# Attention's pipeline one step shorter, its normalisation moved within VectorE's step, in a fused attention and mixture-of-experts kernel on one Trainium2 core

## What is computed

```python
# x, ctx: (64, 64, 128); 16 heads of 8; 8 experts, hidden 512
q, k, v = proj(layernorm(x), Wq, bq), proj(ctx, Wk, bk), proj(ctx, Wv, bv)
q, k = rope(q), rope(k)
p = softmax(where(mask == 0, -1e9, q @ k.T / sqrt(8)))
x = x + tanh(g_xattn) * ((p @ v) @ Wo.T + bo)

z = layernorm(x)
logits = z @ Wr + br
e = argmax(logits);  gate = softmax(logits)[e]
x = x + tanh(g_ffn) * gate * (gelu(z @ W1[e] + b1[e]) @ W2[e] + b2[e])
```

## Time and profile before

| | |
|---|---|
| median of 3 runs | 305.37 us (304.95 to 306.65) |
| the profiled execution | 306.31 us, its span 304.5 us |
| mean granted clock of TensorE | 0.945 of full |
| PE busy | 244.9 us, 80% of the span |
| PEld busy | 210.9 us, 69% |
| DVE busy | 191.4 us, 63% |
| POOL busy | 181.8 us, 60% |
| ACT busy | 166.4 us, 55% |

### The profile page before, as it was taken

The page is one execution under the profiler, slowest core; times in us unless marked ns, Lnnn a source line. Parts: engine busy times, 40 slices in busy tenths (PEclk is TensorE's granted clock), DMA queues, the critical chain, the costliest instruction groups (busy, mean ns, idle before and its releaser), DMA issues.

```text
span 304.5 us, 10523 instructions
## 1 busy us (share of the span) xinstructions
PE 244.9 (80%) x3529; PEld 210.9 (69%) x3529; DVE 191.4 (63%) x639; ACT 166.4 (55%) x481; POOL 181.8 (60%) x222
## 2 busy tenths in 40 slices
PE   1458799997998878888889868869568999999960
PEld 1246687786787766777768656758458899999960
DVE  5546777988798799977797784645623443334420
ACT  2155688886787775778678661342503344444410
POOL 7466567567478875688968764056463455544450
PEclk9999999997999999999999995897787999999995
DMA  7711465464344734152422213310323322100100
GB/s 222 213 17 31 99 199 137 98 174 122 94 140 112 194 68 127 20 151 39 145 44 44 43 39 94 80 41 33 93 87 96 106 67 62 51 29 30 37 19 0
DMA packets 58535, 26.63 MB, mean 87 GB/s; under 512 B 38608, under 2 KB 53989, under 8 KB 58484
## 3 DMA queue, kind: packets, MB, share of 16 engines
q1 hardware_dynamic: 55204, 20.15, 26.9%
q0 software_dynamic: 2272, 4.46, 4.4%
q10 hardware_dynamic: 1008, 1.35, 1.5%
HBM read 16.70 MB, written 5.51 MB: 73 GB/s over the span
## 4 chain that ended last, share of the span: by engine, by line
PE 39%; DVE 13%; issue 13%; POOL 12%; SPq 7%; ACT 6%; DMA 4%; another core or an unknown queue 4%; POOLq 1%; DVEq 0%; ACTq 0%
PE ps L745 11%; SPq L406 5%; PE ps L788 4%; PE ps L729 3%; POOL rot L545 3%; POOL rot L539 3%; PE ps L803 2%; POOL rot_s L541 2%; PE ps L727 2%; PE ps L728 2%; DMA kbd<-kT 2%; DVE mx L1210 2%; PE ps L778 2%; PE ps L830 2%
## 5 line engine op out<-in xcount | busy, mean ns | idle before, releaser
L560 POOL DMA_INDIRECT out<-fin,got x39 | 37.8, 970 | 40.5 <-DVE fin L1259 28.5
L1210 DVE TENSOR_REDUCE mx<-ps 128x16 f16<-128x1024 f32 x32 | 39.1, 1222 | 18.5 <-PE ps L803 14.5
L745 PE MATMUL ps<-w_f,hT 128*128 x312 | 47.5, 298 | 0.0
L512 POOL DMA_INDIRECT rows<-x_all,dest_i x32 | 33.2, 1037 | 21.9 <-DVE x_all L1060 14.7
L1259 DVE SCALAR_TENSOR_TENSOR fin<-ps,got 128x128 f32<-128x128 f32 x39 | 13.7, 350 | 49.2 <-PE ps L745 34.6
L745 PEld LDWEIGHTS ps<-w_f,hT 128*128 128x128 f32 x312 | 40.2, 202 | 1.2 <-issue 0.2
L788 PE MATMUL ps<-vx,pr 128*64 128x32 f32 x1024 | 37.6, 228 | 4.1 <-ACT pr L589 1.7
L788 PEld LDWEIGHTS ps<-vx,pr 128*64 128x64 f32 x1024 | 34.1, 143 | 8.0 <-issue 2.8
L589 ACT ACTIVATE pr<-ps 128x1024 f32<-128x1024 f32 x32 | 32.7, 1022 | 9.4 <-PE ps L830 9.0
L539 POOL TENSOR_TENSOR rot<-qk,cf 128x256 f32<-128x256 f32 x32 | 23.4, 732 | 22.6 <-ACT qk L609 16.0
L657 ACT ACTIVATE hT<-ps 128x512 f32<-128x512 f32 x39 | 23.3, 597 | 22.6 <-PE ps L729 15.3
(11 more groups left out here) (156 smaller groups left out, 606.9 us busy)
## 6 DMA issues: line engine op xcount, KB each, us to landing
kbd<-kT SPq DMA_DIRECT2D x128, 32.0 KB
got<-rows SPq DMA_DIRECT2D x39, 72.0 KB
w_f<-in_W_rows SPq DMA_DIRECT2D x8, 256.0 KB, 2.9
w_r<-in_W_last_row SPq DMA_DIRECT2D x8, 256.0 KB, 3.3
w_f<-in_L_ffn_W SPq DMA_DIRECT2D x8, 256.0 KB, 5.0
x_all<-in_x SPq DMA_DIRECT2D x3, 512.0 KB, 4.9
xt_all<-in_x_t SPq DMA_DIRECT2D x3, 512.0 KB, 4.4
ct_all<-in_ctx SPq DMA_DIRECT2D x3, 512.0 KB, 4.3
```

Source lines behind the costliest of these rows:

```text
L512: pool.indirect_dma_start(out=rows, out_offset=bass.IndirectOffsetOnAxis(ap=dest_i[:, t:t + 1], axis=0), in_=x_all[:, t, :], in_offset=Non ...
L560: pool.indirect_dma_start(out=out_d, out_offset=bass.IndirectOffsetOnAxis(ap=got_i[:, u % GOT, R_ID:R_ID + 1], axis=0), in_=fin[:, u % FRI ...
L745: mm = pe.matmul(o, hT[:, par, c, :], w2_f[:, bass.ds(e, 1), c, :].rearrange("p o n -> p (o n)"), start=False, stop=(c == FC - 1))
L1210: dve.tensor_reduce(mx[:, t % 2, 0:H], ps_s[:, :].rearrange("p (h k) -> p h k", k=S), AX.X, ALU.max).then_inc(mx_done, 1)
```

## The change

Attention's tail is a step shorter: the pair (L1142, L1145) of tile t, its transpose, copy and output projection are in step t+4, with pv, and the output addition and statistics in step t+5. On VectorE the pair moves from ahead of L1155 to behind the statistics L1178 and ahead of the routing pieces. `GROUP_AT` is a step earlier (10, 17, 24, 31, 36), and the scatters with it; F0 stays at 34. The expert number of a tile is worked out ahead of the second layer, a step sooner, and held in a register. The second layer waits for `f_fin` only for the first six tiles and the last. The output bias (once, in step 4) moves ahead of its first use.

```diff
         def out_step(u):
-            return F0 + 5 + u // 2 if u < 3 else min(max(SCATTER_AT) - 2 + u, STEPS - 1)
+            return F0 + 4 + u if u < 2 else min(max(SCATTER_AT) - 1 + u, STEPS - 1)
...
-        GROUP_AT = {b - 1 + 6: g for g, (a, b) in enumerate(GROUPS)}
+        GROUP_AT = {b - 1 + 5: g for g, (a, b) in enumerate(GROUPS)}
...
-        SCATTER_AT = {**{i: 1 for i in (*range(15, 21), *range(22, 32))}, 32: 4, 36: 3, 37: 2, 38: 2, 41: 3, 42: 2}
+        SCATTER_AT = {**{i: 1 for i in (*range(14, 20), *range(21, 32))}, 32: 3, 35: 3, 36: 2, 37: 2, 40: 3, 41: 2}
...
 # ScalarE
-                t = i - 5
+                t = i - 4
                 if live(t):
                     act.wait_ge(onT_done, t + 1)
...
 # TensorE
-                experts[u] = (words[v // PACK] >> (3 * (v % PACK))) & 7
+                experts[u] = pe.snap((words[v // PACK] >> (3 * (v % PACK))) & 7)
...
             def rows_transposed(u):
-                expert_numbers(u)
...
             def second_layer(u):
-                wait(pe, f_fin, used(y_bank, u))
+                if u < 6 or u == NS - 1:
+                    wait(pe, f_fin, used(y_bank, u))
...
             def step(i):
-                t = i - 5
+                t = i - 4
                 if live(t):
                     pe.wait_ge(on_done, t + 1)
...
-                t = i - 5
+                t = i - 4
                 if live(t):
                     pe.wait_ge(onT_ev, t + 1)
                     pe.matmul(ps_op, pick, c_h[:, :], start=True, stop=False)
                     pe.matmul(ps_op, onT[:, t % 2, :], wo_x[:, :], start=False, stop=True).then_inc(op_done, 1)
+                if tile(i - F0):
+                    expert_numbers(i - F0)
                 if tile(i - F0 - 2):
                     second_layer(i - F0 - 2)
...
 # VectorE
-                t = i - 5
-                if live(t):
-                    dve.wait_ge(pv_done, t + 1)
-                    dve.reciprocal(rden[:, t % 2, :], o_ps[:, :, HD]).then_inc(rden_done, 1)
-                    dve.tensor_tensor(on[:, t % 2, :]...)
                 t = i
                 if live(t):
                     dve.scalar_tensor_tensor(out=qk[:, t % 2, 0:D], in0=ps_q, ...)
...
-                t = i - 6
+                t = i - 5
                 if live(t):
                     dve.bn_stats(st6b[:, t % 2, :], x_all[:, t, 0:D]).then_inc(bn2_s, 1)
                     dve.bn_aggr(x_all[:, t, R_MEAN:R_MEAN + 2], st6b[:, t % 2, :]).then_inc(bn2_a, 1)
+                if i == 4:
+                    output_bias_halves()
+                t = i - 4
+                if live(t):
+                    dve.wait_ge(pv_done, t + 1)
+                    dve.reciprocal(rden[:, t % 2, :], o_ps[:, :, HD]).then_inc(rden_done, 1)
+                    dve.tensor_tensor(on[:, t % 2, :]...)
                 if i in GROUP_AT:
                     route_var(GROUP_AT[i])
```

More of the change, by code:

```diff
@@ L806, in step @@
                     mm.then_inc(s_done, 1)
-                t = i - 5
+                if i == 4:
+                    pe.wait_ge(s_prep, 5)
+                    pe.wait_ge(s_wow, 2)
+                    pe.wait_ge(s_idw, 1)
+                    pe.matmul(bank[4][:, P:P + QX], c_bc[:, :], id_wr[:, :], start=True, stop=True).then_inc(s_c, 1)
+                t = i - 4
                 if live(t):
-                    if t == 0:
-                        pe.wait_ge(s_cs, 2)
                     pe.wait_ge(on_done, t + 1)
@@ L834, in step @@
                 if i - 2 in GROUP_AT:
-                    if live(i - 5):
-                        pe.wait_ge(onT_ev, i - 4)
+                    if live(i - 4):
+                        pe.wait_ge(onT_ev, i - 3)
                     else:
@@ L839, in step @@
                     rank_of(GROUP_AT[i - 2])
-                t = i - 5
+                t = i - 4
                 if live(t):
+                    if t == 0:
+                        pe.wait_ge(s_cs, 2)
                     pe.wait_ge(onT_ev, t + 1)
@@ L852, in step @@
                     pe.transpose(ps_mx, mx[:, t % 2, :], ident_h).then_inc(mxT_done, 1)
-                if i == 4:
-                    pe.wait_ge(s_prep, 5)
-                    pe.wait_ge(s_wow, 2)
-                    pe.wait_ge(s_idw, 1)
-                    pe.matmul(bank[4][:, P:P + QX], c_bc[:, :], id_wr[:, :], start=True, stop=True).then_inc(s_c, 1)
             pipeline(step)
@@ L1136, in step @@
                                       ).then_inc(f_lo, 1)
-                t = i - 5
-                if live(t):
-                    dve.wait_ge(pv_done, t + 1)
-                    wait(dve, on_done, t - 1)
-                    o_ps = ps_o.rearrange("p (h c) -> p h c", c=16)
-                    dve.reciprocal(rden[:, t % 2, :], o_ps[:, :, HD]).then_inc(rden_done, 1)
-                    dve.wait_ge(rden_done, t + 1)
-                    wait(dve, onT_done, t - 1)
-                    dve.tensor_tensor(on[:, t % 2, :].rearrange("p (h d) -> p h d", d=HD), o_ps[:, :, 0:HD],
-                                      rden[:, t % 2, :].rearrange("p (h o) -> p h o", o=1).broadcast_to([P, H, HD]),
-                                      ALU.mult).then_inc(on_done, 1)
                 t = i
@@ L1178, in step @@
                     dve.bn_aggr(x_all[:, t, R_MEAN:R_MEAN + 2], st6b[:, t % 2, :]).then_inc(bn2_a, 1)
+                if i == 4:
+                    output_bias_halves()
+                t = i - 4
+                if live(t):
+                    dve.wait_ge(pv_done, t + 1)
+                    wait(dve, on_done, t - 1)
+                    o_ps = ps_o.rearrange("p (h c) -> p h c", c=16)
+                    dve.reciprocal(rden[:, t % 2, :], o_ps[:, :, HD]).then_inc(rden_done, 1)
+                    dve.wait_ge(rden_done, t + 1)
+                    wait(dve, onT_done, t - 1)
+                    dve.tensor_tensor(on[:, t % 2, :].rearrange("p (h d) -> p h d", d=HD), o_ps[:, :, 0:HD],
+                                      rden[:, t % 2, :].rearrange("p (h o) -> p h o", o=1).broadcast_to([P, H, HD]),
+                                      ALU.mult).then_inc(on_done, 1)
                 if i in GROUP_AT:
@@ L1227, in step @@
                     output_bias()
-                if i == 4:
-                    output_bias_halves()
                 if i == 20:
```

## The result

The changed kernel takes **313.21 us** (median of 4 runs, 312.66 to 314.08); the kernel before, on the same chip, 305.9 us. The ratio is 1.022, 95% interval 1.015 to 1.029: slower, as forecast, and by 7.3 us where 4.4 were forecast. The profiled execution took 312.66 us with a span of 310.8 us, 6.3 more than before's 304.5.

What follows compares the result with a forecast made beforehand. The prediction took a loop of waits to bound attention and TensorE the expert layers. Attention +9.3, joint -2.0 and expert tiles -2.9 gave +4.4 us: 309.8 us from a median of 305.37, range 303 to 316.5, the forecast's own 307 to 313.

Steps and rivals of the forecast that it cites:

- the loop that the forecast called tight: Attention: stack transposes, pv, score matmuls, VectorE's maximum, casts and GpSimd's L526 form one gapless loop of 4.76 us in step 8.
- No engine in the loop rests between its input and its start: Attention loop, step 8: anything put between pv's end and the maximum lengthens the step by its own length.
- The pair and the statistics behind pv: VectorE in attention: the pair adds 0.5 us a step (14.0 us), input statistics about 0.45 us (10.0 us), before deductions.
- TensorE's next halt takes it in: nothing: TensorE in attention: the product's transpose starts later, but the halt at the maximum's transpose absorbs it; cost nothing.
- stay at about 5: Attention sign: plain steps without input statistics (24 on) stay at about 5 us; those with go from 4.8 to 5.3.
- Routing pieces: VectorE in attention's routing steps: operations behind the pair cost 2.7 us per group, 8.3 us in all before deductions.
- Rival 2: Routing operations stretch inside GpSimd's rotation, adding 4 to 7 us: 314 to 317 us; sign L973, L1001 over 1 us; chance 0.17.
- The attention sum of +9.3: Attention: work put between pv's end and the maximum, 33.7 us, less what already lay there, leaves +9.3 us.
- The joint, -2.0: Between attention and expert tiles: one attention step fewer saves 2.0 us, between 1.0 and 2.9.
- One wait per expert tile: TensorE's second layer: one semaphore wait fewer saves 0.09 us for 32 tiles, -2.9 us, ends 0 and -4.8.
- The clock, rival 3: Longer TensorE halts in attention's routing steps lose its clock, 4 us more: 313 to 314 us; chance 0.08.
- no one's: Joint: the rest of TensorE's stop has no cause in the waits; a shrink over 5 us would prove this wrong.

Runs made afterwards that it cites:

- 9, swap: Kernel before with ScalarE's copy of the transposed maximum (L595) moved ahead of the exponential (L589); ratio to before 1.003 (1.000 to 1.006).
- experiment 6: Kernel before with VectorE's reciprocal and product for the step's own tile right in front of the maximum, TensorE's order untouched; ratio 1.015 (1.008 to 1.022).
- experiment 1: Changed kernel with reciprocal and product moved behind input statistics and routing pieces, right in front of the maximum; 1.025 of before, 299.2 us against 291.5.
- experiment 7: Kernel before with the step's own reciprocal and product ahead of routing pieces and input statistics, TensorE's order untouched; ratio 1.021 (1.016 to 1.025).
- experiment 8: Kernel before with TensorE's transpose of the product (L815) also waiting for ScalarE's third value copy (L637); ratio 1.015 (1.010 to 1.021).
- 2: Kernel before with only the second layer's wait on the final sum left out where it is implied; ratio 0.990 (0.985 to 0.994).
- 3: Kernel before with VectorE's routing pieces also waiting for the step's pv, reciprocal and product left at the step's head; ratio 1.014 (1.009 to 1.018).
- 12: Changed kernel with its late scatters spread over steps 35 to 42 and held until their step's tile is reached; 1.017 of before (1.010 to 1.024).
- 4: Kernel before with GpSimd's 16 late row scatters spread over steps 36 to 43 and held for their step's tile; ratio 0.996 (0.993 to 1.000).
- 10: Kernel before with expert-tile wait left out, late scatters spread, and ScalarE's copy ahead of the exponential, all together; ratio 0.983 (0.977 to 0.989).
- 11: Kernel before with late scatters spread over steps 36 to 43, run again in a third set; ratio 0.994 (0.990 to 0.997).

## Why the prediction was right, and where it was not

**Two paths, not one.** The stack transposes L778 wait for both GpSimd's L526 and ScalarE's copy L595. From L778's start to the end of the pv behind it are 1.66 us (56.12 to 57.78). Ahead of L778 stand two paths, and the runs of step 8 give both (us, from the rows above and the earlier trace rows; the L815 of before started at 53.39, the swap's L815 and maximum at 53.98 and 54.09, and experiment 6 has them at 53.94 and 54.11 and L778 at 56.66):

| kernel | product's transpose to L778 | maximum to L778 | step, L778 to L778 |
|---|---|---|---|
| before | **2.73** | 2.62 | 4.76 |
| changed | **2.73** | **2.45** | 5.08 |
| 1, pair last | **2.72** | 2.85 | 5.07 |
| 6, pair last, TensorE untouched | **2.72** | 2.55 | 4.76 |
| 7, VectorE's half | 3.05 | **2.46** | 5.08 |
| 8, TensorE's half | **2.70** | 3.07 | 5.21 |
| 9, swap | 2.59 | **2.48** | 4.62 |

In each row the path that is at its shortest (bold) is the one that sets the step; the other has slack. (In the swap the transpose's path is shorter than elsewhere, since the copy no longer stands behind the exponential.) In the kernel before it was the transpose's: 0.37 us behind pv, plus 2.73, plus 1.66, is 4.76. The maximum's would have allowed 0.48 + 2.46 + 1.66 = 4.60, the length of steps 22 and 29; with the transpose's path shortened by the swap, step 8 comes to 0.48 + 2.48 + 1.66 = 4.62. So the loop that the forecast called tight had 0.16 us of slack, and another path, which it did not see, had none. In the changed kernel they are level: 0.69 + 2.73 + 1.66 = 5.08 and 0.97 + 2.46 + 1.66 = 5.09. This is why undoing one of them alone gave nothing.

The forecast's points in its order:

- **"No engine in the loop rests between its input and its start"** failed for L778. The profile names L526 as its releaser; L526 ended at 55.88 and L595 at 55.86. TensorE started 0.26 us after L595. In experiments 1 and 8, where L526 had long been done, it is 0.25 and 0.26; behind L526 it is 0.10 in the changed kernel, in 7 and in 9. Two releasers 0.02 us apart are no evidence for either.
- **The pair and the statistics behind pv**: right in length (0.97 us, experiment 7 too). The first 0.16 us put there cost nothing, because of that slack: 0.33 us for 0.49. Experiment 7 alone gives 6.1 of the 7.6 us that the maximum of step 31 is later.
- **"TensorE's next halt takes it in: nothing"** is the step that failed in mechanism. TensorE has no halt there to give: the sixteen matmuls behind the transpose feed the exponential. Alone it would cost 0.32 us in a plain step (experiment 8: 0.45 for 0.47). In steps with input statistics it cost nothing on top, since VectorE's path had become as long. In steps 28 to 30, which have none, it sets the step by itself: the maximum starts only 0.54 to 0.66 us behind pv, yet from L778 to L778 they take 5.07 or 5.08 us, 4.93, 4.76 and 4.84 before (experiment 7: 4.76 and 4.75 in steps 29 and 30). The profile names the copy there:

```profile
174.70 1.22 DVE L1214 TENSOR_REDUCE mx<-ps 128x16 f16<-128x1024 f32 x1
174.73 0.33 PE L818 MATMUL ps<-cf,on 128*128 128x128 f32 x1
176.41 0.67 POOL L526 TENSOR_TENSOR stk<-rot,stk 128x256 f16<-128x256 f32 x1 [1.07 <-DVE stk L1226]
177.46 0.61 PE L778 MATMUL ps<-ch,stk 128*128 128x128 f16 x8 [0.31 <-ACT mxT L595]
```

  The forecast's sign that these steps would "stay at about 5" was not far off in number, but it had no cause for their getting longer.
- **Routing pieces**, 8.3 us before what was taken off. The 16 steps of 5 to 31 that carry them in either kernel (10 to 14, 17 to 21, 24 to 28, 31) sum to 89.7 us before and 91.0 after, the other 11 to 54.1 and 57.9. So 3.8 of the 5.1 us are the plain loss of 0.34 us a step, and routing costs 1.3. Rival 2 would have put 4 to 7 us there. Its sign, L973 and L1001 at over 1 us, went the other way: L1001 (now L1003) takes 274 ns on the mean instead of 676, the longest L973 (now L975) 0.71 us instead of the 1.09 of the earlier trace rows.
- **Step 4**, 2.0 us longer (7.34 for 5.30), was not foreseen, and it is one-time. The output bias's halves (L934, L936) now stand ahead of the pair, and VectorE waited 1.53 us for TensorE's L811:

```profile
34.54 0.29 DVE L934 CAST c_h<-ps 64x136 f16<-64x136 f32 x1 [1.53 <-PE ps L811]
```

  The attention sum of +9.3 came near 7.9 because this missing term and the slack that the sum left out have opposite signs, which is luck.
- **The joint, -2.0**, is the term that came out wrong in the total. In the sets where before takes 291 to 292 us, it came with the forecast's sign, by one profile of each: 30.2 us (experiment 1) with the shorter pipeline, 32.2 to 34.0 (experiments 2, 3, 9) without; with the scatters spread 29.8 (12) and 30.4 to 31.5 (4, 10, 11). Where it takes 306 to 307 us, before and experiments 6 to 8 have 43.0 to 43.3 and the changed kernel 43.7 and 44.1. So here the step was given back. One of the waits of that stretch, in the last step of attention, is:

```profile
212.67 0.26 DVE L1177 RECIPROCAL rden<-ps 128x16 f32<-128x16 f32 x1 [6.05 <-remote]
```

  pv is shown from 206.50 to 207.62, but the reciprocal that needs it starts at 212.67; in experiment 1 the same wait is 1.06 us. The kernel before has such waits too, whose releaser the profile calls "remote", at other places:

```profile
186.29 1.22 DVE L1210 TENSOR_REDUCE mx<-ps 128x16 f16<-128x1024 f32 x1 [3.80 <-remote]
228.76 0.35 DVE L1259 SCALAR_TENSOR_TENSOR fin<-ps,got 128x128 f32<-128x128 f32 x1 [5.96 <-remote]
```

  All six profiles from the sets of 306 to 307 us have them between 185 and 240 us, the longest 6.2 to 7.5 us, and none of the eight from the faster sets has one. They go with the long joint, whichever kernel runs. The granted clock over 185 to 235 us is 0.83 in the changed kernel and 0.79 in before; in experiments 1, 2 and 12 it is 0.93 to 1.00. Whether that is a cause or goes with the stops is not shown. The reading of before's stop as "no one's" was fair, and so was the warning that it may come again elsewhere. What stops TensorE there is **not settled**: bursts of scatters are my guess, and no run with them spread comes from such a chip.
- **One wait per expert tile**: right in mechanism and size. 0.086 us a tile measured (1.955 to 1.869) for 0.09, and experiment 2 shows it alone. The Trainium skill's rule (Perfetto Trace Analysis, Identifying Dependency Chains) that a further wait may need an instruction of its own gave no price; the runs put it at 0.08 to 0.09 us here. That it is such an instruction, no trace shows.
- **The clock, rival 3**: in attention no stretch lost it. From 50 to 180 us the changed kernel has a granted clock of 1.00, with TensorE busy 110.6 of 130 us, and before 0.99 (50 to 170 us, 105.0 of 120):

```profile
50.00:180.00 130.00, 110.62 (x1934) 89.97 (x1931) 100.85 (x316) 92.81 (x292) 92.49 (x119) 1.00 0.41 102
...
185.00:235.00 50.00, 33.16 (x423) 28.65 (x423) 24.64 (x103) 17.04 (x36) 23.48 (x25) 0.83 0.24 66
```

  The Trainium skill's rule that a less active TensorE may lose its clock (TensorE: Matmul & The Clock Gate, What's actually happening) would have made attention slower than the sum; no run of this case shows it for halts of this length (mostly 0.25 us a step ahead of L818).

The total, 313.2 us for a forecast of 309.8, lay inside the range of 303 to 316.5 and just outside the forecast's own of 307 to 313, but not because each term held: attention came 1.4 us shorter than summed, the joint 2.7 us longer, and the two errors inside attention hid each other.

## What to carry to other kernels

Before pricing what a change puts on one path of a loop, write down every path that meets at the same waiting instruction, with its slack. Where two inputs of a wait end within a few hundredths of each other, the releaser that the profile names is a guess, and a kernel that delays one of them by a known amount settles it. A pipeline that is made one step shorter turns "ready since the last step" into "needed in this one" on each engine that it touches; count what is queued behind each such wait, also on the engine where the moved work is not. When two paths are level, undoing one shows nothing (experiment 1), so test the halves one at a time in the kernel before and not in the changed one.

## What the runs showed of the hardware that I had not expected

- TensorE starts later behind ScalarE than behind GpSimd: 0.25 to 0.26 us after the end of L595 (before, experiments 1 and 8), 0.10 us after the end of L526 (changed, 7 and 9).
- One wait less on TensorE's queue gives 0.08 to 0.09 us per expert tile in a stretch where it is busy 19.9 of 20 us.
- The same program takes 5% longer on one chip than on another (307.0 and 291.4 us for the kernel before), and most of the difference is at the joint, 43.0 us from the last maximum to the ninth tile against 32.2 to 34.0 (experiments 2, 3 and 9); another 2.5 to 4.2 us lie in attention's last two steps (14.3 us from the maximum of step 31 to that of step 33 against 10.1 to 11.9). It goes with waits of 1.6 to 6.2 us for a "remote" releaser in the profile of before, of which experiment 2 has none, and with a granted clock over 185 to 235 us of 0.79 against 0.97. A change that works there must be measured on more than one.
